# DRAM scratch of q and k laid out as row groups read it

## What is computed

```
q, k, v = x @ wq, x @ wk, x @ wv          # 16 query heads, 4 key heads, 16 wide
q, k    = rope(q), rope(k)
p       = softmax(q @ k.T / 4)            # each key head serves 4 query heads
x       = layernorm(x + (p @ v) @ wo)
h       = silu(x @ Wg.T) * (x @ Wu.T)     # W = (int - 128) * scale, 1024 wide
out     = layernorm(x + h @ Wd.T)
```

## Time and profile before

| | us |
|---|---|
| median of 3 runs | 1015.37 (1012.94 to 1015.94) |
| the profiled execution | 1014.48 |
| its span | 1012.7 |
| TensorE busy | 947.9 (94%) |
| VectorE busy | 822.5 (81%) |
| ScalarE busy | 696.4 (69%) |
| GpSimd busy | 237.3 (23%) |
| share of the DMA queue of SP | 26.2% of 16 engines' span |

### The profile page before, as it was taken

One profiled execution on the slowest core, in us unless ns is written; L12 is line 12 of the kernel. 1 busy time (PEld: TensorE's weight loads), 2 busy tenths in 40 slices (PEclk: granted clock), 3 DMA queues, 4 the chain that ended last, 5 costly groups with the idle time before them and its releaser, 6 DMA issues.

```text
span 1012.7 us, 15932 instructions
## 1 busy us (share of the span) xinstructions
PE 947.9 (94%) x5632; PEld 475.1 (47%) x5632; DVE 822.5 (81%) x1601; ACT 696.4 (69%) x878; POOL 237.3 (23%) x162
## 2 busy tenths in 40 slices
PE   7886999999999999999999999999997899999985
PEld 3343433333333333333333333333336787777774
DVE  2756689999999999999999999999833678877756
ACT  1324588998999899989989898999983333433332
POOL 9874274000000000000000000000002445544433
PEclk9886589999999999999999999999999999999997
DMA  5667443142232332332323313301201010011001
GB/s 158 207 215 156 146 104 103 33 78 71 52 68 61 73 67 47 83 67 51 79 53 69 68 41 73 87 24 46 73 8 53 21 42 18 25 42 43 22 21 42
DMA packets 48450, 70.65 MB, mean 70 GB/s; under 512 B 15152, under 2 KB 27184, under 8 KB 48368
## 3 DMA queue, kind: packets, MB, share of 16 engines
q1 hardware_dynamic: 47552, 66.45, 26.2%
q0 software_dynamic: 816, 3.15, 1.0%
HBM read 46.47 MB, written 16.25 MB: 62 GB/s over the span
## 4 chain that ended last, share of the span: by engine, by line
PE 66%; DVE 13%; issue 4%; POOL 4%; ACT 4%; POOLq 0%; DVEq 0%; ACTq 0%
PE pv_bank L971 24%; PE ring_bank L948 24%; DVE block_max L607 8%; PE pair_bank L1021 7%; PE pair_bank L1071 6%; POOL hid_l L528 3%; PE pv_bank L1080 2%; ACT probs L867 2%; DVE hid L758 1%; PE ring_bank L1080 1%; DVE x L675 1%; POOL rstd L513 1%; ACT hid_h L883 1%; PE ring_bank L987 1%; ACT silu L893 1%
## 5 line engine op out<-in xcount | busy, mean ns | idle before, releaser
L867 ACT ACTIVATE probs<-pair_bank 128x1024 f32<-128x1024 f32 x512 | 495.6, 1024 | 48.9 <-PE pair_bank L1021 48.9
L607 DVE TENSOR_REDUCE block_max<-ring_bank 128x1 f32<-128x512 f32 x720 | 467.1, 684 | 41.1 <-PE ring_bank L948 30.0
L948 PE MATMUL ring_bank<-k_max,q_sb 64*128 64x512 f32 x1024 | 348.2, 487 | 18.6 <-DMA q_sb<-q_parts 7.8
L948 PEld LDWEIGHTS ring_bank<-k_max,q_sb 64*128 64x128 f32 x1024 | 144.8, 191 | 301.6 <-DVE block_max L607 151.8
L971 PE MATMUL pv_bank<-probs,v_sb 128*32 128x512 f32 x2048 | 273.6, 606 | 1.4 <-ACT probs L867 1.3
L1021 PE MATMUL pair_bank<-q_sb,k_sb 64*128 64x512 f32 x1024 | 251.6, 425 | 1.8 <-ACT probs L867 1.8
L509 POOL TENSOR_TENSOR attn<-attn,inv_rows 128x1024 f32<-128x1024 f32 x8 | 19.5, 2438 | 532.9 <-DMA inv_rows<-inv_d 532.9
L1021 PEld LDWEIGHTS pair_bank<-q_sb,k_sb 64*128 64x128 f32 x1024 | 117.8, 186 | 31.9 <-ACT probs L867 15.7
L893 ACT ACTIVATE silu<-pair_bank,gate_s 128x512 f32<-128x512 f32 x64 | 44.1, 689 | 125.3 <-PE pair_bank L1071 125.2
L528 POOL TENSOR_TENSOR hid_l<-hid,hid_h 128x512 fp32r<-128x512 f32 x64 | 84.7, 1329 | 143.8 <-ACT hid_h L883 143.8
L838 ACT ACTIVATE above<-ring_bank 128x512 f32<-128x512 f32 x152 | 90.6, 598 | 34.5 <-PE ring_bank L948 31.4
(11 more groups left out here) (95 smaller groups left out, 879.4 us busy)
## 6 DMA issues: line engine op xcount, KB each, us to landing
q_sb<-q_parts SPq DMA_DIRECT2D x192, 64.0 KB, 2.3
k_max<-k_parts SPq DMA_DIRECT2D x96, 96.0 KB, 3.2
k_sb<-k_parts SPq DMA_DIRECT2D x96, 64.0 KB, 2.4
x_in<-xT SPq DMA_DIRECT2D x8, 512.0 KB, 5.0
q_parts<-high SPq DMA_DIRECT2D x16, 256.0 KB, 4.4
q_parts<-low SPq DMA_DIRECT2D x16, 256.0 KB, 4.7
attn<-pv_sb SPq DMA_DIRECT2D x128, 32.0 KB
inv_rows<-inv_d SPq DMA_DIRECT2D x64, 64.0 KB, 2.3
```

Of the source, the lines that this page charges most:

```text
L607: dve.reduce_max(block_max[half % 2][:, col:col + 1], bank[:], axis=AX.X).then_inc(ring_used, 1)
L867: act.activation(probs[t % 2][:, 2 * pr:2 * pr + 2, :], pair_bank[pr][:], ACT.Exp, scale=D ** -0.5).then_inc(probs_ready, 1)
L948: pe.matmul(bank[:], q_sb[k][rows, i, qt * P:(qt + 1) * P], k_max[k // QH][rows, kind * CH:(kind + 1) * CH], start=True, stop=True).then_i ...
```

## The change

The scratch gets another layout. `q_parts` becomes one block for each of the 64 heads, with its high part and its low part behind each other. `k_parts` becomes (combo, half of the head dimension, key head, 8 rows, columns): the three combos of a key head are stored, so the high part is written twice (`K_COMBOS`).

- Stores of q are as many and as large as before, at other addresses.
- Stores of k: one transfer of 64 rows for each combo, so three of 128 KB in place of four of 64 KB, for each chunk and for the gap.
- Loads of k (`k_max`, `k_sb`): one transfer of 48 rows for each group, two in place of six.
- Loads of q: one of 32 rows and one of 16 rows for each group, four in place of six.
- The counts on the semaphores follow.

The diff, cut to its core:

```diff
-        q_parts = nc.dram_tensor("q_parts", (2, PAIRS, UNITS, G * D, S), fp32).ap()
-        k_parts = nc.dram_tensor("k_parts", (2, B * HKV, D, S + CH), fp32).ap()
+        q_parts = nc.dram_tensor("q_parts", (B * H, 2, D, S), fp32).ap()
+        k_parts = nc.dram_tensor("k_parts", (COMBOS, 2, B * HKV, HALF, S + CH), fp32).ap()
...
             def load_q(pair, k):
                 s, qh = k // QH, k % QH
                 for r in range(GROUPS):
-                    for combo in range(COMBOS):
-                        src = q_parts[Q_PART[combo], pair, s].rearrange("(j r) t -> r j t", r=D)
-                        row = r * GROUP + combo * D
-                        sp.dma_start(q_sb[k][row:row + D].bitcast(fp32), src[:, 2 * r:2 * r + 2, qh * CH:(qh + 1) * CH]).then_inc(q_loaded[k], 16)
+                    head = (UNITS * pair + s) * G + 2 * r
+                    src = q_parts[head:head + 2, :, :, qh * CH:(qh + 1) * CH]
+                    row = r * GROUP
+                    sp.dma_start(q_sb[k][row:row + 2 * D].bitcast(fp32), src.rearrange("j c r t -> (c r) j t")).then_inc(q_loaded[k], 16)
+                    sp.dma_start(q_sb[k][row + 2 * D:row + ROWS].bitcast(fp32), src[:, 0].rearrange("j r t -> r j t")).then_inc(q_loaded[k], 16)
 
             def load_k(dst, pair, s, done):
+                width = S + CH if dst is k_max else S
                 for r in range(GROUPS):
-                    for combo in range(COMBOS):
-                        row = r * GROUP + combo * D
-                        part = k_parts[K_PART[combo], 2 * pair + s]
-                        sp.dma_start(dst[s][row:row + D].bitcast(fp32), part if dst is k_max else part[:, 0:S]).then_inc(done[s], 16)
+                    src = k_parts[:, :, UNITS * pair + s, :, 0:width].rearrange("c f r t -> (c f) r t")
+                    sp.dma_start(dst[s][r * GROUP:r * GROUP + ROWS].bitcast(fp32), src).then_inc(done[s], 16)
...
-                                dst = k_parts[part, bass.ds(HKV * b, HKV)]
-                                for half in range(2):
-                                    src = buf[slot][half * 32:half * 32 + 32, :]
-                                    sp.dma_start(dst[:, half * HALF:(half + 1) * HALF, cols], src.bitcast(fp32)).then_inc(stored[slot], 16)
+                                store_k(part, b, cols, buf[slot], stored[slot])
...
+            def store_k(part, b, cols, buf, done):
+                for combo in K_COMBOS[part]:
+                    dst = k_parts[combo, :, HKV * b:HKV * (b + 1), :, cols].rearrange("f h r t -> f (h r) t")
+                    sp.dma_start(dst, buf[0:HKV * D, :].bitcast(fp32)).then_inc(done, 16)
```

More of the change, by code:

```diff
@@ L26 @@
 ROWS = COMBOS * D
-Q_PART, K_PART = (0, 0, 1), (0, 1, 0)
-TERMS = 16 * GROUPS * COMBOS
+Q_LOADS = 16 * GROUPS * 2
+K_LOADS = 16 * GROUPS
+K_COMBOS = ((0, 1), (2,))
 SHIFT = 2
@@ L230, in stores @@
         def stores(slot):
-            return 16 * 2 * (1 if slot % QK < 2 else 2)
+            return 16 * (2 if slot % QK < 2 else COMBOS)
         def each(n, body):
@@ L282, in projections @@
                         sp.wait_ge(stored[slot], stores(slot))
-                    sp.wait_ge(gap_stored, 64)
+                    sp.wait_ge(gap_stored, 16 * COMBOS)
                     sp.wait_ge(v_used, 2)
@@ L301, in projections @@
                             if j < 2:
-                                dst = q_parts[part, bass.ds(2 * b, 2)].rearrange("q s (j r) t -> (q s j) r t", r=D)
-                                sp.dma_start(dst[:, j * HALF:(j + 1) * HALF, cols], buf[slot][:].bitcast(fp32)).then_inc(stored[slot], 16)
-                            else:
-                                dst = k_parts[part, bass.ds(HKV * b, HKV)]
-                                for half in range(2):
-                                    src = buf[slot][half * 32:half * 32 + 32, :]
-                                    sp.dma_start(dst[:, half * HALF:(half + 1) * HALF, cols], src.bitcast(fp32)).then_inc(stored[slot], 16)
+                                dst = q_parts[H * b:H * (b + 1), part, j * HALF:(j + 1) * HALF, cols]
+                                sp.dma_start(dst, buf[slot][:].bitcast(fp32)).then_inc(stored[slot], 16)
+                            else:
+                                store_k(part, b, cols, buf[slot], stored[slot])
                 store_gap(b)
+            def store_k(part, b, cols, buf, done):
+                for combo in K_COMBOS[part]:
+                    dst = k_parts[combo, :, HKV * b:HKV * (b + 1), :, cols].rearrange("f h r t -> f (h r) t")
+                    sp.dma_start(dst, buf[0:HKV * D, :].bitcast(fp32)).then_inc(done, 16)
             def store_gap(b):
@@ L314, in store_gap @@
                     sp.wait_ge(ready, b + 1)
-                    dst = k_parts[part, bass.ds(HKV * b, HKV)]
-                    for half in range(2):
-                        sp.dma_start(dst[:, half * HALF:(half + 1) * HALF, S:S + CH], buf[half * 32:half * 32 + 32, :].bitcast(fp32)).then_inc(gap_stored, 16)
+                    store_k(part, b, slice(S, S + CH), buf, gap_stored)
             each(B, projections)
@@ L323, in _ @@
                 sp.wait_ge(stored[slot], stores(slot) * B)
-            sp.wait_ge(gap_stored, 64 * B)
+            sp.wait_ge(gap_stored, 16 * COMBOS * B)
             sp.wait_ge(v_used, 2 * B)
@@ L485, in _ @@
                 pool.wait_ge(stored[slot], stores(slot) * B)
-            pool.wait_ge(gap_stored, 64 * B)
+            pool.wait_ge(gap_stored, 16 * COMBOS * B)
             pool.wait_ge(v_used, 2 * B)
@@ L576, in key_gap @@
                 if b:
-                    dve.wait_ge(gap_stored, 64 * b)
+                    dve.wait_ge(gap_stored, 16 * COMBOS * b)
                 dve.tensor_tensor(gap[:], rotated_k[0][0:HKV * D], rotated_k[1][0:HKV * D], ALU.subtract).then_inc(gap_ready, 1)
@@ L822, in gap_high @@
                 if b:
-                    act.wait_ge(gap_stored, 64 * b)
+                    act.wait_ge(gap_stored, 16 * COMBOS * b)
                 act.activation(gap_h[:], gap[:], ACT.Copy).then_inc(gap_h_ready, 1)
@@ L956, in _ @@
             for k in range(2):
-                pe.wait_ge(q_loaded[k], TERMS)
+                pe.wait_ge(q_loaded[k], Q_LOADS)
                 if k == 0:
-                    pe.wait_ge(kmax_loaded[0], TERMS)
+                    pe.wait_ge(kmax_loaded[0], K_LOADS)
                 for e in range(MAXES):
@@ L1009, in attention @@
                             if k % QH == 0:
-                                pe.wait_ge(kv_loaded[s], (TERMS + 16) * (p + 1))
+                                pe.wait_ge(kv_loaded[s], (K_LOADS + 16) * (p + 1))
                         if t == 0 and more:
-                            pe.wait_ge(q_loaded[x], TERMS * p + (TERMS if k < 2 else 2 * TERMS))
+                            pe.wait_ge(q_loaded[x], Q_LOADS * p + (Q_LOADS if k < 2 else 2 * Q_LOADS))
                             if k % QH == 0:
-                                pe.wait_ge(kmax_loaded[x // QH], TERMS * p + (TERMS if k < 2 else 2 * TERMS))
+                                pe.wait_ge(kmax_loaded[x // QH], K_LOADS * p + (K_LOADS if k < 2 else 2 * K_LOADS))
                         def scores(pr):
```

## The result

| | before | after |
|---|---|---|
| median, us | 1013.41 (6 runs) | 1063.07 (6 runs, 1059.92 to 1065.67) |
| the profiled execution | 1014.48 | 1065.67 |
| its span | 1012.7 | 1063.8 |
| share of SP's DMA queue, of 16 engines' span | 26.2% | 21.7% |

The ratio is 1.0483, 95% interval 1.0460 to 1.0505: slower by 4.8%. The median of before is that of six runs; the 1015.37 given earlier was of the first three.

A forecast was written before the change was run, and what follows sets the result against it. It took two DMA engines, filled by stores of k, to bound the projections and delay the scores: 1014.5 us, 0 for saved issues, plus 48 gives 1062.5 us, range 1045 to 1092.

The forecast's parts named there:

- share and rate with stores of k alone: Windows where only stores of k move: two engines, a share near 0.13 and 49 GB/s.
- a batch of the projections, `x_in` to `x_in`: Projections: engines 0 and 1 carry 32.1 us of transfers for each batch that took 18.0.
- first maxima: Start of attention: the maxima begin at 128 us instead of 89.06, after the first `k_max` and q land.
- scores begin: Loop of scores: begins at 173 us instead of 124.94, 48 us later, once the shift has landed.
- Rate of an engine: All transfers before the scores: each DMA engine moves 24.5 GB/s, read from windows with stores on four engines.
- the ledger: Engine 0's transfers, taken as never idle: 92.2 us ahead of attention's first loads, so 120.7; last stores done at 168.1.
- Loads on six engines: Attention's loads up to its first shift: 345 kB on engine 0, taken as 18 us, between 14.1 and 34.
- The shift: Before the scores: issued 2.0 us after SP's release, landing some 2.3 later, so 4.3 in all, at 173.
- nothing behind takes it back: Loop of scores: it is TensorE's own, so the 48 us idle ahead of it stays in the total.
- No change through four engines: Rival: stores of k keep four engines, 20.1 us a batch; +2 to 3 us, 1017; chance 0.04.
- The faster one, sixteen engines everywhere: Rival: transfers spread over sixteen engines, or other two each time; 7 us gained, 1007; chance 0.06.
- Slower through the loads all along attention: Rival: loads of k stay at 10 GB/s an engine throughout attention; 1090 to 1110 us; chance 0.04.

The follow-up runs named there:

- k16_stores: The changed kernel with its scratch of k laid out batch first, so a store's 64 rows are one dimension; 1012.84 us, 1.0016 of the kernel before.
- spread_all: The changed kernel with k's columns ordered half, row, head and a scratch to match, stores and loads both on sixteen engines; 1011.03 us, 0.9977 of before.
- late_weights: The changed kernel with GpSimd's first weight load waiting until the first shift has landed; 1058.83 us, 1.0446 of the kernel before.
- k4_stores: The changed kernel with a head-first scratch of k: stores of 4x8x512 on four engines, 48-row loads in one dimension; 1015.27 us, 1.0042 of before.
- copy_alone: The kernel before with the high part of k stored a second time in the old four-engine form, never read; 1017.55 us, 1.0053 of before.

## Why the prediction was right

**The time**: 1062.5 us foretold, a median of 1063.07 measured, inside the forecast's own bounds. The mechanism is the one that was named: stores of k on two engines, which hold up everything behind them. Its steps, each with what it came to:

| step | foretold | measured |
|---|---|---|
| share and rate with stores of k alone | 0.13, 49 GB/s | 0.13, 51 GB/s |
| a batch of the projections, `x_in` to `x_in` | 32.1 us | 32.0 |
| `x_in` from issue to landing | 10 us or more | 12.2 |
| first maxima | 128 | 131.45 |
| SP released | 168.6 | 169.19 |
| scores begin | 173 | 177.00 |
| attention itself | as before | 550.80 busy of 560 |

**The sum was closer than its terms, and part of that is luck.** Three of them were off. Two largely cancel; the third does not, and the scores begin 4 us later than foretold. The profiled execution shows it, at 1065.67, 3.2 over the forecast. The median lies 2.6 below that execution, and the forecast started from an execution 1.1 above the median of before. From median to median the change costs 49.7 us, where 48 were foretold.

- *Rate of an engine*, 24.5 GB/s from the four-engine rows: the two-engine rows give 25.5. The projections' share of the ledger, 92.2 us, becomes 88.6, and the window of 114 to 116 us is the last with a share near 0.13 (0.15, 57 GB/s), where the ledger had 120.7.
- *Loads on six engines*, 18 us for 345 kB, "near the fast end". Worked back: 28.2 us of stores at 25.5 GB/s before the release at 169.2 leave the loads ending near 141, so up to 25 us, the middle of the stated 14 to 34; by the windows below four of the six engines are through with them at 139. The reason given for the fast end did not hold. k16_stores shows the cost without a backlog: 14.4 us to the first matmul where spread_all, with sixteen engines, takes at most 8.4. The two errors, some -4 and +5 to +7, largely cancel by the release (169.19 for 168.6).
- *The shift*, 4.3 us from issue to landing, taken from a load of q that shared the engines with nothing. It took 7.8, and late_weights shows half of that to be GpSimd, which is released by the same stores and puts 1 MB of weights on the engines half a microsecond later: with that load held back, 3.9 us are left. In the kernel before GpSimd's load follows SP's at the same distance (115.10 behind 114.56), so the shift was there probably 2 to 3 us ahead of its use and not 6; no row gives its landing.

The span grew by 51.1 for 52.1 at the scores, so the step "nothing behind takes it back" held to 1 us, as far as two single executions can tell; the change's runs lie up to 6 us apart.

**The rivals.** No change through four engines (1017) is what k4_stores and copy_alone ran, at 1015.27 and 1017.55. The faster one, sixteen engines everywhere at 1007, is spread_all: 1011.03. Its mechanism is real, but of the 7 us put on it 2 arrived: TensorE's waits at the maxima, 6.26 and 2.42 us, are there for ScalarE and no longer for a load. Slower through the loads all along attention fell: TensorE is as busy there as before.

**Where it could have gone wrong** was in the mean DMA share. 0.26 in a window with one kind of transfer in it said four engines, and the written side's leading 4 said why. The Trainium skill's rule ("DMA: Bandwidth & Descriptors", the section on why a DMA increments its semaphore by 16) gave two and six for the change. The share of 0.13 agrees for the two. For the six two places agree. In steady attention of k16_stores, whose loads of k have the change's shape, SP issues `k_max` from 208.66 and `k_sb` from 210.25, and this window has their data alone:

```profile
211.00:212.50 1.50, 1.50 (x13) 0.62 (x12) 1.47 (x5) 1.50 (x2) 0.00 (x0) 1.00 0.37 135
```

That is six of sixteen (0.375), 22.5 GB/s each. The same loads in spread_all, on sixteen engines:

```profile
207.00:208.50 1.50, 1.50 (x14) 0.46 (x6) 1.50 (x4) 1.50 (x3) 0.00 (x0) 1.00 1.10 238
```

And in the change itself the backlog is one of six engines here, before it is one of two (the window of 158 to 160 shown above):

```profile
136.00:138.00 2.00, 2.00 (x5) 1.01 (x4) 1.12 (x5) 1.20 (x2) 0.00 (x0) 0.50 0.38 145
```

The same page of the Trainium skill has a rule of size (measured bandwidth: larger transfers run closer to peak), which pointed the other way. Here the 128 KB stores ran at 51 GB/s and the 64 KB ones before at 98: the number of engines decided. What size gives at an equal number of engines, no run here shows.

## What to carry to other kernels

Before merging transfers, write down the slowest dimension of both sides as the instruction will carry it. Here a leading 4, 6 and 2 gave shares of 0.26, 0.37 and 0.13, so four, six and two engines of sixteen, and the transfers that spread over all of them queued behind (`x_in`, 5.0 us to landing before and 12.2 after). Add up the busiest engine's bytes, not the mean: a mean share of 0.13 was a full queue. When a layout has to change, order it so that the rows of a store and of a load each have a single step, as spread_all does by permuting a weight's columns. In this kernel that undid the whole loss, but gained only 0.2% over the kernel before.

## What the runs showed of the hardware that was not expected

- SP's issue of a transfer, 0.4 to 0.6 us when the engines keep up, took 2.42 to 4.49 us when two engines were behind (rows above, at 46.47, 48.97 and 153.78): a store of 65.5 kB on one engine takes 2.57 at 25.5 GB/s. So it looks as if SP itself is held until such a store has drained; that was not tested, nor how many transfers may be outstanding.
- A load of 48 rows costs SP more to issue on six engines than on sixteen: 1.70 us for the first two `k_max` in k16_stores, 0.82 in spread_all. The forecast had 0.45 us for every issue.
- Four small copies of the shift, 4 KB each, took 7.8 us beside 1 MB of weights on the same engines, and 3.9 without.
- Loads on six engines cost 6 us at the start of attention against sixteen (14.4 against at most 8.4), though the kernel before, with 16-row loads on sixteen engines and three times as many issues of `k_max`, needed only 8.8. By themselves the six run at 22.5 GB/s each, near the 24.5 and 25.5 of the stores, so it is their number that limits such a window. What holds them up further at the start of attention, where loads of q share the engines, was not separated.
